# A cross-attention block with routed experts: shared matrices split by GpSimd piece by piece, output bias added early, second inverse root from a power on GpSimd

## What is computed

```python
x = x + tanh(g_xattn[0]) * xattn(layernorm(x), ctx, ctx, group_prob, mask, wq, bq, wk, bk, wv, bv, wo, bo)
x = x + tanh(g_ffn[0])   * ffn(layernorm(x), nw, router, sw1, sb1, sw2, sb2, ew1, eb1, ew2, eb2)

def xattn(query, key_in, value, group_prob, mask, ...):   # 16 heads of 16 columns
    q, k, v = heads(query @ wq + bq), heads(key_in @ wk + bk), heads(value @ wv + bv)
    logits = q @ k.T / sqrt(16) + (1 - mask) * -1e9
    attn = softmax(logits) * group_prob
    return merge(attn @ v) @ wo + bo

def ffn(h, ...):
    normed = h * rsqrt(mean(h * h) + 1e-08) * nw
    shared = relu(normed @ sw1 + sb1) @ sw2 + sb2
    probs = sigmoid(normed @ router.T)                    # 8 experts, the best 2 per token
    return shared + routed(normed, probs, ew1, eb1, ew2, eb2)
```

## Time and profile before

| | us |
|---|---|
| median of 3 runs | 665.79 |
| the 3 runs | 665.79, 665.81, 664.26 |
| the profiled execution | 664.07 |
| its span, first to last instruction | 662.3 |

### The profile page before, as it was taken

The page is one execution under the profiler, slowest core; times in us unless marked ns, Lnnn a source line. Parts: engine busy times, 40 slices in busy tenths (PEclk is TensorE's granted clock), DMA queues, the critical chain, the costliest instruction groups (busy, mean ns, idle before and its releaser), DMA issues.

```text
span 662.3 us, 18982 instructions
## 1 busy us (share of the span) xinstructions
PE 582.3 (88%) x6006; PEld 491.5 (74%) x6006; DVE 437.8 (66%) x1190; ACT 430.8 (65%) x1072; POOL 296.4 (45%) x329
## 2 busy tenths in 40 slices
PE   2689999999999999999976699999999999999950
PEld 2457787778777877788754588888888888888840
DVE  5957878777778877877868675456554535535327
ACT  4378787788887887888772656547465655756330
POOL 8403434334444433334554007784476545558110
PEclk9799999999999999999998589999999999999985
DMA  8534556775655555563205004214455743552228
GB/s 232 146 101 129 143 136 169 203 203 145 152 138 143 114 135 128 140 152 88 72 1 181 11 1 139 101 48 127 145 160 111 192 120 104 135 153 60 52 73 308
DMA packets 106456, 84.28 MB, mean 127 GB/s; under 512 B 42595, under 2 KB 100197, under 8 KB 106286
## 3 DMA queue, kind: packets, MB, share of 16 engines
q1 hardware_dynamic: 103374, 75.59, 43.6%
q0 software_dynamic: 3040, 8.16, 3.5%
HBM read 50.45 MB, written 28.30 MB: 119 GB/s over the span
## 4 chain that ended last, share of the span: by engine, by line
PE 64%; DVE 6%; ACT 3%; issue 3%; POOL 2%; DMA 2%; ACTq 0%; POOLq 0%; SPq 0%; DVEq 0%
PE ps L1083 18%; PE ps L1096 17%; PE ps L949 9%; PE ps L967 5%; PE ps L936 4%; PE ps L902 3%; PE ps L878 3%; ACT probs L750 1%; PE ps L1071 1%; DVE kT L1198 1%; DVE x_sb L1453 1%; PE ps L866 1%; DMA probs<-x_sent 1%; DVE x_sb L1452 1%; DVE arena L1317 1%
## 5 line engine op out<-in xcount | busy, mean ns | idle before, releaser
L949 PE MATMUL ps<-ident,probs 112*125 112x112 f32 x768 | 192.6, 277 | 2.4 <-POOL probs L548 1.4
L750 ACT ACTIVATE probs<-probs,negmax 112x375 f32<-112x375 f32 x256 | 154.9, 608 | 25.9 <-DVE negmax L1245 25.8
L949 PEld LDWEIGHTS ps<-ident,probs 112*125 112x125 f32 x768 | 139.0, 188 | 23.5 <-issue 7.3
L1245 DVE CUSTOM_DVE_ANT_0 probs<-ps,neg 112x375 f32<-112x375 f32 x256 | 137.2, 537 | 12.7 <-issue 10.1
L800 ACT ACTIVATE arena<-ps,b 128x256 f32<-128x256 f32 x192 | 79.2, 463 | 100.9 <-PE ps L1083 100.9
L548 POOL TENSOR_TENSOR probs<-probs,gp_in 112x375 f32<-112x375 f32 x64 | 58.5, 915 | 179.7 <-ACT probs L750 179.6
L1096 PE MATMUL ps<-w,arena 128*128 128x256 f16 x1152 | 129.8, 273 | 0.0
L1252 DVE TENSOR_TENSOR arena<-ps,gpT 125x336 f32<-125x336 f32 x192 | 96.9, 505 | 46.1 <-PE ps L949 45.6
L1385 DVE TENSOR_TENSOR arena<-arena 128x512 f16<-128x512 f32 x96 | 74.9, 787 | 73.4 <-ACT arena L805 73.1
L1096 PEld LDWEIGHTS ps<-w,arena 128*128 128x128 f16 x1152 | 112.4, 98 | 13.3 <-DVE arena L1385 0.2
L1083 PE MATMUL ps<-probs,w 128*128 x816 | 92.1, 273 | 1.3 <-DMA probs<-x_sent 0.6
(11 more groups left out here) (170 smaller groups left out, 789.0 us busy)
## 6 DMA issues: line engine op xcount, KB each, us to landing
k_scratch<-kT SPq DMA_DIRECT2D x96, 93.8 KB
kst<-k_scratch SPq DMA_DIRECT2D x64, 140.6 KB, 3.5
w1s<-in_L_ffn_ew_dram SPq DMA_DIRECT2D x8, 1024.0 KB, 5.2
w2s<-in_L_ffn_ew_dram SPq DMA_DIRECT2D x8, 1024.0 KB, 5.8
x_sent<-y_sb SPq DMA_DIRECT2D x12, 516.0 KB, 5.1
ctx_in<-in_ctx_dram SPq DMA_DIRECT2D x16, 375.0 KB
arena<-y_back SPq DMA_DIRECT2D x7, 512.0 KB, 6.8
q_scratch<-qT SPq DMA_DIRECT2D x24, 112.0 KB
```

The lines of the kernel that those rows point to most:

```text
L750: act.activation(probs[:, n % PROBS], probs[:, n % PROBS], ACT.Exp, bias=negmax[:, p, n:n + 1], scale=-1.0, accum_out=rowsum[:, p, ORDER[n ...
L949: mm = pe.transpose(ps[0:KP, PT[n % 2], c * S:(c + 1) * S], probs[:, n % PROBS, c * KP:(c + 1) * KP], ident[0:S, 0:S])
L1245: dve.tensor_tensor_reduce(probs[:, n % PROBS], bank(SC[n % 2], S, S2), neg[:, p], -1.0, BIG, ALU.add, ALU.min, negmax[:, p, n:n + 1]).the ...
```

## The change

There are three edits.

1. **Shared matrices.** ScalarE's high parts (L773, L775) and GpSimd's two low parts (L612, L614) are gone. In their place GpSimd makes both parts in eight pieces of 128 x 512, each a cast and a subtraction (`split_shared`). They stand in batches 11, 12 and 13, behind the work for n = 2, n = 8 and n = 12: three in batch 11, three in batch 12, two in batch 13. GpSimd's loop is cut to batches 5 to 10 for that, and 11 to 13 are written out. SP's wait for the two low parts is unchanged, and is met from batch 13 on.
2. **Output bias.** The seven additions move from batches 14 and 15 to batches 1 to 4, behind the work for n = 2 and n = 8.
3. **Second inverse root.** ScalarE's Sqrt (L777) and the load of its table are gone. GpSimd raises a to the power -0.5 in one `tensor_tensor` against a tile `half` that holds -0.5 (14 elements on each of 128 partitions), and VectorE refines the result y as y * (1.5 - 0.5 * a * y * y), in four instructions in place of five. The first inverse roots stay on ScalarE.

```diff
@@ -178,7 +178,7 @@
-        dve_ask, act_ask, act_gave = sem("dve_ask"), sem("act_ask"), sem("act_gave")
+        dve_ask, act_gave, pool_gave = sem("dve_ask"), sem("act_gave"), sem("pool_gave")
@@ -586,32 +591,56 @@
-                    if not more:
-
-                        part = (k + (len(POOL_HEADS) if last else 0)) * BIAS_TILES
-                        if part < NT:
-                            tiles = slice(part, min(part + BIAS_TILES, NT))
-                            pool.tensor_tensor(x_sb[:, tiles], x_sb[:, tiles],
-                                               bo_bc[:, :].unsqueeze(1).to_broadcast([P, tiles.stop - part, D]), ALU.add).then_inc(resid, 1)
+                    if isinstance(t, int) and 1 <= t <= QC and k in (0, 2):
+                        add_out_bias(2 * (t - 1) + k // 2)
+                    if isinstance(t, int) and t > QC and k != 1:
+                        split_shared((t - SPLIT_FROM) * 3 + (k + 1) // 2)
+            def split_shared(n):
+
+                if n >= 2 * W_CUTS:
+                    return
+                first, k = n < W_CUTS, n % W_CUTS
...
+                pool.tensor_copy(high, of).then_inc(sw_hi, 1)
+                pool.wait_ge(sw_hi, n + 1)
+                pool.tensor_tensor(low, of, high, ALU.subtract).then_inc(sw_lo, 1)
+                if k == W_CUTS - 1:
+                    pool.wait_ge(sw_lo, n + 1)
+                    pool.sem_inc(w1_hi if first else w2_hi, 1)
+                    pool.sem_inc(w1_lo if first else w2_lo, 1)
...
-            pool.wait_ge(w1_hi, 1)
-            pool.tensor_tensor(w1[:, 0, LO], w1s[:, :, :], w1[:, 0, HI], ALU.subtract).then_inc(w1_lo, 1)
-            pool.wait_ge(w2_hi, 1)
-            pool.tensor_tensor(w2[:, 0, LO], w2s[:, :, :], w2[:, 0, HI], ALU.subtract).then_inc(w2_lo, 1)
...
+            pool.wait_ge(half_made, 1)
+            pool.wait_ge(dve_ask, 3)
+            pool.tensor_tensor(nrm[:, 1], nrm[:, 0], half[:, :], ALU.pow).then_inc(pool_gave, 1)
@@ -769,12 +801,6 @@
-            act.wait_ge(in_w1, 16)
-            act.activation(w1[:, 0, HI], w1s[:, :, :], ACT.Copy).then_inc(w1_hi, 1)
-            act.wait_ge(in_w2, 16)
-            act.activation(w2[:, 0, HI], w2s[:, :, :], ACT.Copy).then_inc(w2_hi, 1)
-            act.wait_ge(dve_ask, 3)
-            act.activation(nrm[:, 1], nrm[:, 0], ACT.Sqrt).then_inc(act_gave, 1)
@@ -1153,6 +1179,13 @@
+            def refine_inverse_root(some):
+
+                then(dve.tensor_tensor(nrm[:, 3, some], nrm[:, 1, some], nrm[:, 0, some], ALU.mult))
+                then(dve.tensor_tensor(nrm[:, 3, some], nrm[:, 3, some], nrm[:, 1, some], ALU.mult))
+                then(dve.tensor_scalar(nrm[:, 3, some], nrm[:, 3, some], -0.5, 1.5, ALU.mult, ALU.add))
+                then(dve.tensor_tensor(nrm[:, 2, some], nrm[:, 1, some], nrm[:, 3, some], ALU.mult))
@@ -1317,7 +1350,8 @@
             center(range(2))
-            inverse_root(4, slice(0, NT))
+            dve.wait_ge(pool_gave, 1)
+            refine_inverse_root(slice(0, NT))
             dve.sem_inc(root_made, 1)
```

More of the change, by code:

```diff
@@ L138, in flamingo_block @@
         mv = sb("mv", [P, NT, 2], F32)
+        half = sb("half", [P, NT], F32)
         nrm = sb("nrm", [P, 8, NT], F32)
@@ L207, in flamingo_block @@
         sb2_added = sem("sb2_added")
+        sw_hi, sw_lo, half_made = sem("sw_hi"), sem("sw_lo"), sem("half_made")
         w1_hi, w1_lo, w2_hi, w2_lo = sem("w1_hi"), sem("w1_lo"), sem("w2_hi"), sem("w2_lo")
@@ L536, in _ @@
             pool.memset(est[:, :, :], 0.0).then_inc(sum_zero, 1)
+            pool.memset(half[:, :], -0.5).then_inc(half_made, 1)
             pool.iota(token_row[:, :], [[2 * P, NT]], base=YPAD, channel_multiplier=2).then_inc(sum_zero, 1)
@@ L567, in split_out @@
                 pool.tensor_tensor(oT[:, LO, :, cols], o32[:, :, :], oT[:, HI, :, cols], ALU.subtract).then_inc(oT_lo, 1)
+            SPLIT_FROM, W_CUTS = B - 5, 4
             def step(t, p, own, ahead, more=True, last=False, first=False):
@@ new lines, in step, with add_out_bias @@
+                    if isinstance(t, int) and t > QC and k != 1:
+                        split_shared((t - SPLIT_FROM) * 3 + (k + 1) // 2)
+            def add_out_bias(n):
+                if n == 0:
+                    pool.wait_ge(bo_made, 1)
+                    pool.wait_ge(xn_made, NT)
+                if n * BIAS_TILES < NT:
+                    tiles = slice(n * BIAS_TILES, min((n + 1) * BIAS_TILES, NT))
+                    pool.tensor_tensor(x_sb[:, tiles], x_sb[:, tiles],
+                                       bo_bc[:, :].unsqueeze(1).to_broadcast([P, tiles.stop - tiles.start, D]), ALU.add).then_inc(resid, 1)
@@ new lines, in split_shared @@
+            def split_shared(n):
+                if n >= 2 * W_CUTS:
+                    return
+                first, k = n < W_CUTS, n % W_CUTS
+                if n == 0:
+                    pool.wait_ge(xn_T, NT)
+                if k == 0:
+                    pool.wait_ge(in_w1 if first else in_w2, 16)
+                if first:
+                    cut = (slice(k // ND, k // ND + 1), slice(k % ND * F // ND, (k % ND + 1) * F // ND))
+                    high, low, of = w1[:, 0, HI, cut[0], cut[1]], w1[:, 0, LO, cut[0], cut[1]], w1s[:, cut[0], cut[1]]
+                else:
+                    cut = slice(k * NF // W_CUTS, (k + 1) * NF // W_CUTS)
+                    high, low, of = w2[:, 0, HI, cut], w2[:, 0, LO, cut], w2s[:, cut]
+                pool.tensor_copy(high, of).then_inc(sw_hi, 1)
[5 more added lines that the diff above has]
+                    pool.sem_inc(w1_lo if first else w2_lo, 1)
@@ L597, in _ @@
             for t in range(QC + 1):
                 step(t, t % 2, t // 2 + 1, (t + 1) // 2 + 1, first=t == 0)
-            with pool.Fori(QC // 2, B // 2 - 2) as i:
+            with pool.Fori(QC // 2, SPLIT_FROM // 2) as i:
                 step(2 * i + 1, 1, i + 1, i + 2)
                 step(2 * i + 2, 0, i + 2, i + 2)
-            step(B - 3, 1, B // 2 - 1, B // 2)
-            pool.wait_ge(bo_made, 1)
-            pool.wait_ge(xn_made, NT)
+            for t in range(SPLIT_FROM, B - 2):
+                step(t, t % 2, t // 2 + 1, (t + 1) // 2 + 1)
@@ L1404, in weigh_pairs @@
             def weigh_pairs():
-                dve.wait_ge(act_gave, 5)
+                dve.wait_ge(act_gave, 4)
                 then(dve.tensor_scalar(top[:, 6:8], top[:, 6:8], 1.0, None, ALU.add))
```

## The result

| | before | changed |
|---|---|---|
| median of 10 runs, us | 664.89 | 667.36 |
| lowest to highest | 662.73 to 666.94 | 665.48 to 669.60 |
| the profiled execution | 664.07 | 665.88 |
| its span | 662.3 | 663.9 |

The ratio is 1.0041, with a 95% interval from 1.0023 to 1.0060: slower by 2.7 us, somewhere from 1.5 to 4.0. (The ratio is not the quotient of the two medians, which lie 2.5 us apart.) The median of 667.36 lies inside the stated range of 663.5 to 667.8. But a ratio of 1.0041 is on the side to which the forecast gave 0.15, slower by over 0.3%, and not in the 0.77 for no change.

The account below looks back on a forecast made before the run. The prediction took the passage after attention to wait for VectorE. Its terms, 0 + 0 - 0.20 - 0.21 + 0.43, sum to +0.02 us on the profiled 664.07, or 665.8 against the median of 665.79; range 663.5 to 667.8.

Parts of the forecast that it names:

- The range: Whole kernel: the predicted median lies between 663.5 and 667.8 us.
- What bounds the kernel: End of attention and passage from 344.5 to 381.2 us: it waits for VectorE, not for work taken off ScalarE or GpSimd.
- The splits leave the passage: 0: Passage after attention: ScalarE's copies and table load and GpSimd's subtractions are hidden by idle time, so removing them gives 0.
- rival (d): Passage and shared tiles: the two removed table loads count, 1.28 us each, -2.56 in all, 663.2 us; chance 0.03.
- The pieces: 0: Batches 11 to 13: a piece of 1.79 us fits GpSimd's 2.03 us idle place behind n = 8; 0, at most 1.5.
- rival (b): Batches 11 to 13: a piece delays the multiplication for n = 12, up to +1.5 us, 667.3; chance 0.08.
- The bias: -0.20: Batch 15: without the bias additions, the next exponentials and n = 12 come 0.20 us earlier; bounds 0 and -0.57.
- The refinement: -0.21: Second inverse root on VectorE: four refining instructions in place of five, at 0.21 us each, save 0.21 us.
- The power: +0.43: Second inverse root: GpSimd's power, taken at 1.0 us, lets VectorE go on 0.43 us later; ends 0 and +3.5.
- rival (a): Second inverse root: slow power, VectorE waits for GpSimd; over 2.0 us slower beyond 3.0 us, +3.1 at 4.08; chance 0.13.
- Rival (c): Passage and first shared block: TensorE's full clock comes back earlier, -2.4 us in all, 663.4; chance 0.05.
- SP: 0: Loads of expert 0: they follow batch 15's keys at once, into staging tiles nobody reads until the shared tiles; costs nothing.

Follow-up runs that it names:

- x5: The kernel before with only the splits moved, as eight GpSimd pieces in batches 11 to 13; 665.93 us, ratio 1.0009 to the kernel before.
- x3: The changed kernel with eight centerings ahead of the wait for the power in place of two; 664.74 us, ratio 1.0009 to the kernel before.
- x12: The changed kernel with the second inverse root back on ScalarE's Sqrt, timed a second time; 664.52 us, ratio 0.9997 to the kernel before.
- x2: The kernel before with only the second inverse root changed to GpSimd's power; 666.32 us, ratio 1.0035 to the kernel before.
- x4: The changed kernel with four more GpSimd powers in the opening, of 14, 14, 1 and 28 elements per partition; one run, span 665.5 us.
- x11: The changed kernel again, unchanged, in a series where every kernel took some 18 us more; 684.85 us, ratio 1.0039 to the kernel before.
- x7: The changed kernel with ScalarE's Sqrt back and SP held so expert 0's matrices load late; 665.68 us, ratio 0.9997 to the kernel before.

## What was right and wrong in the prediction, point by point

**The range** held, the forecast of no change (+0.02 us) did not, and that the range held was luck in part. The prediction starts from 665.79, the median of three runs; ten runs of the same kernel have 664.89. On the higher start the measured 2.5 to 2.7 us would have given 668.3 to 668.5, beyond the range's end of 667.8.

**What bounds the kernel** was right. The passage waits for VectorE, root included, and what was taken off ScalarE and GpSimd there gave nothing that can be seen.

**The splits leave the passage: 0** was right. ScalarE's idle time grew from 11.37 to 19.99 us, and x5 shows no gain. With that, rival (d) falls. It wanted 2.56 us back for the two table loads. x3 has neither of them and doesn't wait for the power, and stands at 1.0009 [0.9996, 1.0023], so at most 0.3 us faster; x12 has both again (at 344.38 and 400.09 us) and stands at 0.9997. What the Trainium skill, ScalarE: Activation LUTs, section "What ACT_TABLE_LOAD costs", states is the price of a switch, not whether anything waits for it. Behind the first load stood 11.37 us of idle time, and beside the second, at 400.63, TensorE was busy without a gap.

**The pieces: 0** was right within 0.1 us. The piece took 1.87 us from 301.48 to 303.35, where 1.79 was taken, and 0.33 us were left; rival (b) wanted the multiplication for n = 12 to come late, and it waits for ScalarE in all three batches (0.31, 0.32 and 0.33 us). What they do cost is 0.1 us: batch 13, from its first multiplication to that of batch 14, takes 18.52 to 18.55 us in every profile with the pieces and 18.43 or 18.44 in every one without.

**The bias: -0.20** had the right sign and place. Counted from the multiplication for n = 6, the one for n = 8 comes 0.57 us earlier, which is the bound, and the one for n = 12 comes 0.32 earlier, where 0.20 was taken; at the last split it is 0.45. The copy that I let hold back n = 12 held it back less. No comparison of times here can show so little.

**The refinement: -0.21** was right: from 361.77 to 362.40 and one pitch more are four instructions at 0.21 us.

**The power: +0.43, taken at 1.0 us. This is the step that failed.** It took 2.75, so the term is +2.18 by its own working (2.75 - 0.57), and VectorE's 2.13 us of idle time are that. It is beyond the 2.6 us at which the forecast's own range ended. The mechanism was rival (a)'s, word for word: VectorE waits for GpSimd, and no other engine's work can hide it. x2 shows that it is enough, x3 that without the uncovered wait the loss goes. Only the size was misjudged. Between the ends 0.22 and 4.08, I went close to the lower, "because the shape is the cast's". The shape is not what this price follows: x4 has 0.158 us per element, where the subtraction of rows 4 has 4.08 / 2048 = 0.002. An operation of another function has no near row. The middle of the bounds, 2.15, would have given +1.2 in place of +0.02, and still been too low.

With 2.75 in place of 1.0 the sum is -0.41 + 2.18 = +1.8 on the profiled execution; by the stages of the traces it is 1.88 - 0.45 + 0.1 = +1.5, which is where the interval of the ratio begins. Rival (a) put its threshold for "slower by over 0.3%" at d = 3.0, above what was measured, so that even the right price would have left the forecast at 667.6, just inside "no change".

Whether anything stands beyond the power is **open**. By the ratios, three comparisons with the power at the old place gave 2.7, 2.3 (x2) and 2.7 us (x11), by the medians 2.5, 1.6 and 2.1. The stages give 1.5 for the change and 1.9 for x2, and each interval takes that in or begins there. For x3, with the power covered, the stages give -0.7 (-0.4 in the root, -0.45 and +0.1 in attention), and its interval begins at -0.3: so a part of the difference between kernels may lie outside these stages. Block 1, the candidate in the first profile with 7.9 us, was 6.4 in x2 and 6.5 in x11, so it isn't that. The mixing at the end takes 12.5 to 13.0 us in all six profiles with the power and 12.4 in all eight with the Sqrt. Why was not tried, and it isn't the answer either: together with the stage ahead of it, it makes 24.5 to 24.7 us in the three profiles of these comparisons, where the two of before have 24.5 and 24.8. No other stage is longer in all three.

**Rival (c)**, the clock, didn't bring its gain; in the profiled execution it went the other way. This is what makes block 1 longer there. One row each for the kernel before, the change and x11, the microsecond in which the granted clock went from 0.50 to 1.00:

```profile
384.00:385.00 1.00, 1.00 (x8) 0.79 (x7) 0.90 (x4) 0.97 (x3) 0.00 (x0) 0.72 0.06 16
386.00:387.00 1.00, 1.00 (x9) 0.85 (x8) 0.90 (x5) 0.97 (x3) 0.00 (x0) 0.85 0.00 0
385.00:386.00 1.00, 1.00 (x11) 0.90 (x10) 0.86 (x5) 0.82 (x2) 0.00 (x0) 0.98 0.07 16
```

A mean of 0.72 puts the step at 384.6, and the others at 386.3 and 385.0. Block 1 starts at 381.2, 380.7 and 382.4, so it ran at 1.2 GHz for 3.3, 5.6 and 2.6 us. Half of that is lost against the 5.24 us of a block at full clock, which gives 6.9, 8.0 and 6.5; measured were 6.9, 7.9 and 6.5. The last two are the same kernel, so the later step of the first profile does not belong to the change. What sets the step's moment was not tried.

**SP: 0** was right: x7 with the late loads and x12 with the early ones both have 0.9997.

## What to carry to other kernels

The price of an operation that the trace doesn't show cannot be taken from the shape of another: leave the whole width between the bounds in the range, or measure it alone in an idle stretch of the same kernel, as x4 does. Work moved between engines is worth nothing where it was hidden, and costs its uncovered remainder where another engine waits for it, here 2.75 us less the 0.57 that stood beside it. Where a serial piece stands ahead of a pipeline that another engine paces, weave it into that pipeline's gaps: this gave 3.2 us in the one series in which it was timed. A range that holds says little when the start that it is laid on is a median of three runs that scatter by more than the terms of the sum.

## What the runs showed of the hardware

- A power on GpSimd, float32 on 128 partitions, costs 0.39 us + 0.158 us per element of a partition (x4; 1, 14 and 28 elements: 0.55, 2.6 and 4.81 us), with nothing that shows for its first use (2.63, then 2.59). In the root, 14 elements took 2.72 to 2.75.
- The Trainium skill, GPSIMD Engine Reference, section "Specifications", names contention with VectorE instructions with two SBUF inputs. Beside eight of those, the power of x3 took 2.74 us, and beside two, in the change, 2.75; this operation shows none of it. A cast took 0.99 us beside such a VectorE instruction and 0.61 otherwise.
- In one series the shared tiles behind block 1 took some 20 us more (89.1 in x11 against 68.6). For about 13 of these TensorE stood still, waiting for nothing that the profile shows: from 390 to 470 us it was busy for 67.1 us of 80 in x11, and for 79.9 in the change's first profile. The rest went with the clock, which fell there to 0.50. The chain of x11:

```profile
426.04 1.16 issue
427.20 0.58 PE ps L1122 x2
...
428.27 1.06 issue
429.33 0.37 PE ps L1122
429.70 1.73 issue
```

  A few matmuls, then a gap of 1 us or more. The ten microseconds from 430, in x11 and in the change's first profile:

```profile
430.00:440.00 10.00, 3.53 (x11) 1.20 (x11) 0.69 (x1) 1.47 (x3) 6.00 (x7) 0.50 0.26 93
430.00:440.00 10.00, 10.00 (x94) 8.95 (x93) 4.24 (x7) 5.07 (x12) 8.39 (x9) 1.00 0.25 90
```

  The other two kernels profiled in that series show the same stage as long (87.8 and 89.7 us). The cause was not tried.
